# Second layer's routing in a fused two-layer kernel: first choice from the logits, weights computed last, half of an addition and of a norm on GpSimd, one dispatch split in two

## What is computed

```python
xn = _layernorm(x)
s  = attention(xn)                 # layer 0: 16 heads, causal
g  = silu(experts_top2(xn))        # layer 0: 8 experts
x  = x + s * g
xn = _layernorm(x)
s  = recurrent_attention(xn)       # layer 1: phases, cumulative sums, MLP
g  = silu(_L1_ffn_ref(xn))         # layer 1: 8 experts, capacity 64 per group of 256 tokens
x  = x + s * g
```

```python
raw = softmax(logits); idx1 = argmax(raw); gate1 = raw[idx1]
rest = raw * (1 - onehot(idx1)); idx2 = argmax(rest); gate2 = rest[idx2]
p1 = cumsum(m1) - m1                    # place of a token in its expert's buffer
p2 = cumsum(m2) - m2 + count(m1)
expert_inputs = einsum('GSEC,GSM->EGCM', dispatch, x)   # one-hot matmul, 8 groups of 256 tokens
```

## Time and profile before

| | us |
|---|---|
| three timed runs | 617.03, 617.17, 614.8; median 617.03 |
| the profiled run, device time | 616.33 |
| its span | 614.5 |
| busy in the span | TensorE 573.1, VectorE 476.7, ScalarE 330.9, GpSimd 190.4 |
| mean granted TensorE clock | 0.981 of full |

### The profile page before, as it was taken

The page is one execution under the profiler, slowest core; times in us unless marked ns, Lnnn a source line. Parts: engine busy times, 40 slices in busy tenths (PEclk is TensorE's granted clock), DMA queues, the critical chain, the costliest instruction groups (busy, mean ns, idle before and its releaser), DMA issues.

```text
span 614.5 us, 11961 instructions
## 1 busy us (share of the span) xinstructions
PE 573.1 (93%) x3901; PEld 352.2 (57%) x3902; DVE 476.7 (78%) x1307; ACT 330.9 (54%) x602; POOL 190.4 (31%) x221
## 2 busy tenths in 40 slices
PE   2878999999999999899999998989899999999996
PEld 1433544444444534899999963535446665656554
DVE  6799889999989898455555578666899899976465
ACT  2762567676777776555555558864223642362224
POOL 1451000000254452133333310000007685688300
PEclk9898899999999999999999999999999999999999
DMA  8955727070813171211111034215011322421412
GB/s 185 210 182 206 241 77 216 3 217 1 224 31 109 53 226 20 56 49 47 47 47 47 26 97 128 71 41 151 0 46 25 97 59 54 130 79 40 126 42 68
DMA packets 55612, 57.99 MB, mean 94 GB/s; under 512 B 8651, under 2 KB 39403, under 8 KB 55515
## 3 DMA queue, kind: packets, MB, share of 16 engines
q1 hardware_dynamic: 51242, 50.56, 29.9%
q0 software_dynamic: 4320, 6.81, 3.5%
HBM read 41.96 MB, written 18.85 MB: 99 GB/s over the span
## 4 chain that ended last, share of the span: by engine, by line
PE 76%; DVE 16%; ACT 4%; issue 2%; DMA 1%; SPq 1%; ACTq 0%; DVEq 0%
PE banks L1689 11%; PE banks L1831 10%; PE banks L1756 8%; PE banks L1778 7%; PE banks L1964 7%; PE banks L1701 6%; PE banks L1953 5%; PE banks L1950 5%; PE banks L2015 4%; DVE banks L1239 4%; DVE mpart L1242 3%; PE banks L1759 2%; ACT arena L809 1%; PE banks L1840 1%; PE banks L1598 1%
## 5 line engine op out<-in xcount | busy, mean ns | idle before, releaser
L809 ACT ACTIVATE arena<-banks 128x512 f32<-128x512 f32 (+1 forms) x304 | 154.3, 583 | 75.1 <-PE banks L1759 40.7
L1239 DVE CUSTOM_DVE_ANT_0 banks<-banks,arena 128x512 f32<-128x512 f32 (+3 forms) x256 | 119.7, 511 | 9.2 <-PE banks L1778 8.3
L1756 PE MATMUL banks<-arena 128*128 128x512 bf16 (+3 forms) x384 | 116.6, 331 | 4.0 <-ACT arena L809 2.8
L1778 PE MATMUL banks<-arena 96*128 96x512 bf16 (+3 forms) x384 | 113.5, 336 | 4.8 <-DVE mpart L1239 2.7
L1242 DVE TENSOR_REDUCE mpart<-banks 128x1 f32<-128x512 f32 x128 | 85.8, 683 | 9.1 <-PE banks L1778 8.1
L1689 PE MATMUL banks<-arena 128*128 128x128 f32 x624 | 76.3, 275 | 1.0 <-ACT arena L743 1.0
L1689 PEld LDWEIGHTS banks<-arena 128*128 128x128 f32 x624 | 72.8, 192 | 1.5 <-ACT arena L743 1.5
L1831 PE MATMUL banks<-arena 128*9 128x512 f32 (+3 forms) x768 | 70.7, 487 | 0.0
L851 ACT ACTIVATE arena<-banks 125x512 f32<-125x512 f32 (+2 forms) x48 | 28.4, 595 | 71.2 <-PE banks L1950 46.2
L1756 PEld LDWEIGHTS banks<-arena 128*128 128x128 bf16 x384 | 37.8, 99 | 49.6 <-issue 23.8
L620 POOL DMA_INDIRECT results<-arena x39 | 37.7, 967 | 77.4 <-DVE arena L1133 77.4
(11 more groups left out here) (295 smaller groups left out, 858.0 us busy)
## 6 DMA issues: line engine op xcount, KB each, us to landing
k_parts<-arena SPq DMA_DIRECT2D x6, 768.0 KB, 8.1
arena<-in_L_ffn_experts_w_dram SPq DMA_DIRECT2D x2, 2048.0 KB, 11.1
arena<-results SPq DMA_DIRECT2D x8, 512.0 KB, 6.6
arena<-k_parts SPq DMA_DIRECT2D x7, 576.0 KB
arena<-q_parts SPq DMA_DIRECT2D x28, 144.0 KB
arena<-in_L_ffn_w_kernel_dram SPq DMA_DIRECT2D x8, 344.0 KB, 3.8
slots<-in_pad_rows_dram SPq DMA_DIRECT2D x1, 2535.0 KB, 12.3
arena<-slots SPq DMA_DIRECT2D x39, 65.0 KB, 1.8
```

Source lines behind the costliest of these rows:

```text
L809: act.activation(Pr[:, r % 4, heads[0]:heads[-1] + 1, 0:n], ring_e[e % 3][:, 0:len(heads) * n].rearrange("p (j c) -> p j c", j=len(heads)) ...
L1239: ins = dve.tensor_tensor_reduce(unmasked, unmasked, tail_mask[:, 512 - n:512], 1.0, -BIG, ALU.add, ALU.max, part[:, at:at + 1])
L1756: ins = pe.matmul(ring_e[e % 3][:, at * n:at * n + n], QK[:, slot, j, 1, P * kt:P * kt + P], QK[:, slot, j, 0, q:q + n], start=True, stop= ...
L1778: ins = pe.matmul(ps[:, at * n:at * n + n], QK[0:TALL, slot, j, 0, P * i:P * i + P], QK[0:TALL, slot, j, 1, 512 * half:512 * half + n], st ...
```

## The change

Six edits are made.

1. `route_max` now also finds the one-hot of the first choice, from the logits and their maximum (the new function `first_equal`, which is `first_max` without its first step).
2. `route_choice` no longer divides the exponentials by their sum. It clears the first choice out of the raw exponentials and takes the second choice from what is left.
3. The weights of the two choices are computed by the new function `route_weights`, behind the four one-hot comparisons of each sequence.
4. The addition into `x1` for chunk 2 of the second sequence goes to GpSimd, which waits for VectorE's product (`ya_half`); VectorE waits for that addition (`x1_half`) before `norm_moments(1)`.
5. The last four of the eight rows of the norm (tiles 12 to 15) go to GpSimd, after `refine`; TensorE's transposes of chunk 3 wait for them (`xn1_last`).
6. On TensorE `dispatch(0)` is split: its first tile goes ahead of the last transposes of the attention, its second between them and the products with the output weights. `places1(1)` goes ahead of the eight one-column products.

```diff
@@ GpSimd
+            pool.wait_ge(Z["ya_half"], 1)
+            half = slice(QT, QT + QT // 2)
+            pool.tensor_tensor(x1[:, half, :], x1[:, half, :], ya[:, half, :], ALU.add).then_inc(Z["x1_half"], 1)
+            pool.wait_ge(Z["refined"], 2)
+            for n in range(QT + QT // 2, NT):
+                ins = pool.tensor_scalar(xn[:, n, :], x1[:, n, :], mv[:, n, 0:1], rstd[:, 2, n:n + 1], ALU.subtract, ALU.mult)
+            ins.then_inc(Z["xn1_last"], 1)
@@ VectorE, norm_rows
                     refine(slice(QT, NT))
+                    dve.sem_inc(Z["refined"], 1)
-                for n in range(QT * b, QT * b + QT):
+                for n in range(QT * b, QT * b + (QT // 2 if b else QT)):
@@ VectorE, routing
             def route_max(b):
-                R, r_, _ = halves(b)
+                R, r_, chosen = halves(b)
                 link(dve.tensor_reduce(r_[0], R[0], AX_X, ALU.max))
                 dve.tensor_tensor(R[1], R[0], over_experts(r_[0]), ALU.subtract).then_inc(Z["gates_d"], 1)
+                first_equal(R[0], r_[0], chosen[0], R[4], r_[4])
             def route_choice(b):
                 R, r_, chosen = halves(b)
                 dve.wait_ge(Z["gates_exp"], 2 + b)
-                link(dve.tensor_reduce(r_[0], R[1], AX_X, ALU.add))
-                link(dve.reciprocal(r_[1], r_[0]))
-                link(dve.tensor_tensor(R[0], R[1], over_experts(r_[1]), ALU.mult))
-                first_max(R[0], r_[0], chosen[0], R[4], r_[4])
-                link(dve.scalar_tensor_tensor(R[1], chosen[0], 0.0, R[0], ALU.is_equal, ALU.mult))
-                first_max(R[1], r_[1], chosen[1], R[4], r_[4])
+                link(dve.scalar_tensor_tensor(R[0], chosen[0], 0.0, R[1], ALU.is_equal, ALU.mult))
+                first_max(R[0], r_[1], chosen[1], R[4], r_[4])
                 dve.sem_inc(Z["selb_ready"], 1)
                 link(dve.scalar_tensor_tensor(R[3], chosen[0], 0.0, chosen[1], ALU.is_equal, ALU.mult))
+            def route_weights(b):
+                R, r_, _ = halves(b)
+                link(dve.tensor_reduce(r_[0], R[1], AX_X, ALU.max))
+                link(dve.tensor_reduce(r_[4], R[1], AX_X, ALU.add))
+                link(dve.reciprocal(r_[5], r_[4]))
+                link(dve.tensor_tensor(r_[0], r_[0], r_[5], ALU.mult))
+                link(dve.tensor_tensor(r_[1], r_[1], r_[5], ALU.mult))
@@ VectorE, the second sequence (route_weights(0) and (1) stand behind the one_hot loops)
-                link(dve.tensor_tensor(ya[:, tiles, :], ya[:, tiles, :], psM[...], ALU.mult))
-                link(dve.tensor_tensor(x1[:, tiles, :], x1[:, tiles, :], ya[:, tiles, :], ALU.add))
+                weighted = dve.tensor_tensor(ya[:, tiles, :], ya[:, tiles, :], psM[...], ALU.mult)
+                if c == 2:
+                    weighted.then_inc(Z["ya_half"], 1)
+                else:
+                    link(weighted)
+                    link(dve.tensor_tensor(x1[:, tiles, :], x1[:, tiles, :], ya[:, tiles, :], ALU.add))
+            dve.wait_ge(Z["x1_half"], 1)
             norm_moments(1)
@@ TensorE
+            dispatch(0, (0,))
             pe.wait_ge(Z["m_free"], READS)
...
+            dispatch(0, (1,))
...
-            for g in range(G1 // 2):
+            for g in range(1, G1 // 2):
                 dispatch(g)
             for c in range(2, 4):
-                pe.wait_ge(Z["xn1_ready"], c + 1)
+                pe.wait_ge(Z["xn1_ready"], 3)
+                if c == 3:
+                    pe.wait_ge(Z["xn1_last"], 1)
...
             phases(2)
+            places1(1, psM[:, 1, :])
             for o in range(2):
...
-            places1(1, psM[:, 1, :])
```

More of the change, by code:

```diff
@@ L373, in build @@
             r_done p2_done mem_set zero_o x2_done wg_ps wg_done el_done sqrt_in sqrt_out
-            y1_done disp_ps disp_sb oh_ready dest_in sin_done u1_ps g1_ps hid1_done act1_done gate_zero tail_zero xn1_ready refined full_sb r1_done rem1_done sum_in aT0_sb xT0_sb ld_vecs ld_iota"""
+            y1_done disp_ps disp_sb oh_ready dest_in sin_done u1_ps g1_ps hid1_done act1_done gate_zero tail_zero xn1_ready refined full_sb r1_done rem1_done sum_in ya_half x1_half xn1_last aT0_sb xT0_sb ld_vecs ld_iota"""
         Z = {n: sem(n) for n in names.split()}
@@ L950, in first_max, with first_equal @@
                 link(dve.tensor_reduce(best, values, AX_X, ALU.max))
+                first_equal(values, best, onehot, t1, t2)
+            def first_equal(values, best, onehot, t1, t2):
                 link(dve.tensor_tensor(t1, values, over_experts(best), ALU.is_equal))
@@ L1338, in _ @@
                             one_hot(g, oh0[:, 2 * g:2 * g + 2, :])
+                        route_weights(0)
             assert next(choice, None) is None and next(positions, None) is None
@@ L1345, in _ @@
                 dve.wait_ge(Z["s_ps"], c - 1)
-                link(dve.tensor_tensor(ya[:, tiles, :], ya[:, tiles, :], psM[:, c % 2, :].rearrange("p (n d) -> p n d", d=D), ALU.mult))
-                link(dve.tensor_tensor(x1[:, tiles, :], x1[:, tiles, :], ya[:, tiles, :], ALU.add))
+                weighted = dve.tensor_tensor(ya[:, tiles, :], ya[:, tiles, :], psM[:, c % 2, :].rearrange("p (n d) -> p n d", d=D), ALU.mult)
+                if c == 2:
[4 more added lines that the diff above has]
+            dve.wait_ge(Z["x1_half"], 1)
             norm_moments(1)
@@ L1358, in _ @@
                 one_hot(g, oh[:, 2 * g - 8:2 * g - 6, :])
+            route_weights(1)
             dve.wait_ge(Z["ld_L1"], 16 * 6)
@@ L1644, in places1, with dispatch @@
                 ins.then_inc(Z["pre_ps"], 1)
-            def dispatch(g):
+            def dispatch(g, tiles=(0, 1)):
                 pe.wait_ge(Z["oh_ready"], g + 1)
                 ps, source = (banks[:, g, :], oh0) if g < G1 // 2 else (psM[:, g % 2, :], oh)
-                for i in range(2):
+                for i in tiles:
                     ins = pe.matmul(ps, xn[:, 2 * g + i, :], source[:, (2 * g + i) % 8, :], start=(i == 0), stop=(i == 1))
-                ins.then_inc(Z["disp_ps"], 1)
+                if tiles[-1] == 1:
+                    ins.then_inc(Z["disp_ps"], 1)
             pe.wait_ge(Z["ld_spread"], 16)
```

## The result

The changed kernel takes 619.41 us (median of 20 runs, 616.85 to 623.51), the kernel before 616.44 (median of 20, 614.61 to 619.24). The ratio is 1.005, with a 95% interval of 1.0035 to 1.0064: 3.0 us slower, at the edge of what the prediction called no change. The forecast was 617.3, with a range of 614.9 to 619.9. The profiled run took 620.83 us (span 619.0), 4.50 more than the profiled run of before; 13 of the 20 runs were faster than it, so it shows more than the typical loss.

What follows compares the result with a forecast made beforehand. TensorE holds 76% of the chain that ended last, nearly without pause from dispatch 4 on. The six edits sum to -0.2 us and the clock adds 1.2: +1.0 on the profiled 616.33, so 617.3, range 614.9 to 619.9.

Steps and rivals of the forecast that it cites:

- likeliest case: All edits plus a fall to half clock partly on phases and dispatches: 617.3 us, range 616.3 to 618.2, chance 0.40.
- First sequence's routing: One-hot steps of the first choice fit into VectorE's wait for the exponential; gain 0.2 us, bounds 0 and 0.33.
- Dispatch 0 in two gaps: Its two tiles just fit TensorE's waits before the last transposes and output products; cost 0.1 us, bounds 0 and 0.4.
- Half of the addition: VectorE loses one 128x512 addition to GpSimd, but the two overlapping additions disturb each other; gain 0.35 us, bounds 0 and 0.7.
- Half of the rows on GpSimd: GpSimd's four norm rows end late and hold up chunk 3's transposes and logits; cost 1.3 us, bounds 1.0 and 1.9.
- Rival (c): VectorE's and GpSimd's norm rows exclude each other, chunk 3 0.9 us later; 617.0 at full clock, 618.2 with fall; chance 0.13.
- Second sequence's routing: On VectorE, ten steps instead of 14 and no 0.32 us wait before the second choice; gain 1.35 us.
- TensorE's order: `places1`, one-column products and two phases take 3.6 us before dispatch 4, so TensorE bounds its start, at 435.6.
- Weights at the end: `route_weights(1)` puts five short VectorE steps, some 1.15 us, ahead of the phases' reading; costs nothing, 0.4 us cover left.
- The clock: Longer light stretch on TensorE makes a 3.4 us fall on phases 0 and 3 and dispatches likely; cost 1.2 us.
- rival (b): The fall lasts twice as long, 6.5 us from about 432 on phases and dispatches, costing 3.2; 619.4 us, chance 0.12.
- the signs that the prediction named: Profile: no TensorE idle ahead of dispatch 4, logits copy 0.8 us later, choices 3.25 behind, half clock within 432 to 440.

Runs made afterwards that it cites:

- a4: Kernel before with only the routing edits, plus the semaphore increment ahead of the norm's rows; 0.9999 of the kernel before, 616.31 us.
- c2: Changed kernel with all eight norm rows back on VectorE, measured a second time; 0.9959 of the kernel before, 614.94 us.
- c4: Changed kernel with the counts (`places1`) behind the one-column products again; 1.0048 of the kernel before, 620.47 us.
- b4: Changed kernel with all norm rows on VectorE and three extra unread 512-column products on TensorE; 0.9992 of the kernel before, 618.66 us.
- a2: Changed kernel with dispatch 0 whole again, behind the output products; 1.0051 of the kernel before, 620.9 us.
- b2: Changed kernel with all norm rows on VectorE and dispatch 0 whole; 0.9975 of the kernel before, 617.67 us.
- a3: Changed kernel with three extra unread 512-column products in TensorE's waits for the norm's rows; 1.0000 of the kernel before, 617.5 us.
- a1: Changed kernel with all eight norm rows back on VectorE, first measurement; 0.9966 of the kernel before, 614.93 us.
- b3: Changed kernel with all norm rows on VectorE and the counts behind the one-column products; 0.9997 of the kernel before, 618.75 us.
- b1: Changed kernel with all norm rows and the whole addition on VectorE, first measurement; 1.0052 of the kernel before, 622.51 us.
- c1: Kernel before with one edit alone, the last four norm rows on GpSimd; 1.0032 of the kernel before, 619.25 us.
- c3: Changed kernel with all norm rows and the whole addition on VectorE, second measurement; 1.0003 of the kernel before, 618.28 us.

## Why the prediction came out as it did

The forecast was +1.0 us, in a range that reached to 619.9, and the measured median is +3.0. The time lies inside the range, but outside the 616.3 to 618.2 of the likeliest case. The parts, in the prediction's order:

- **First sequence's routing**, forecast -0.2. The last transposes of the lists start at 411.67 instead of 411.90: -0.23. This pair agrees, but it is not shown by more than the pair: a4, c2, c4 and b4, which have the edit too, have them at 411.55 to 412.16, and the kernel before stands in the middle of that.
- **Dispatch 0 in two gaps**, forecast 0.1. The last transposes of the attention start at 413.05 and the output products at 414.87, 0.05 later than a shift of 0.23 gives. Right, and a2 and b2 show that the split is worth nothing else.
- **Half of the addition**, forecast -0.35. GpSimd's step took 1.27 us (1.155 in rows 6) and VectorE's own 0.97 (0.69 before): the two did disturb each other. The moments begin 2.62 us behind VectorE's first product, 0.27 sooner than before (2.89). The Trainium skill's rule of a full block (SBUF — State Buffer, "Who interferes with whom") would have made VectorE's step end at GpSimd's end plus its own 0.69, 418.18 + 0.69 = 418.87; it ended at 418.72, so this trace comes near the rule without meeting it, and GpSimd, which had begun first, was slowed too.
- **A wait that the prediction left out.** `dve.sem_inc(refined)` stands ahead of VectorE's rows, which now start 0.23 us after the last short step, where they started 0.04 after it: 0.2 us. a4, which has this wait and both additions on VectorE, shows it alone (its row at 422.96 above has the same 0.23): 8.20 us from the first output product to T instead of 8.01. It eats most of the addition's gain, which is 0.27 by itself (8.20 to 7.93); T came out 0.08 earlier, not 0.35.
- **Half of the rows on GpSimd**, forecast T + 3.6 for their end and T + 6.0 for the logits. They ended at T + 3.1 (422.73 + 3.17), four steps of 0.79 and a start of 0.16 behind `refine`, with no disturbance beyond VectorE's four rows taking 1.28 us in place of 1.07. Rival (c), rows that exclude each other, did not happen. The transposes started at T + 3.25, and the logits nevertheless came at T + 6.5, since the 8-column products ran at half clock. With the clock full, in a3, they came at T + 5.6, which is the delay's own price: 0.9 us more than before, where the forecast was 1.3.
- **Second sequence's routing**, forecast -1.35. From the copy of the logits to the end of the second one-hot it is 3.18 us in place of 4.59: -1.4. Right; but TensorE's order let none of it through until the counts were moved (a4).
- **TensorE's order**, forecast 3.6 us from the counts to dispatch 4 at full clock. It was 3.8 to 3.9 in a1, b2 and c2. TensorE is the bound there, as forecast, and VectorE's one-hot no longer waited for.
- **Weights at the end**, forecast nothing: the experts waited for the copy of the last dispatch. Right; in a4 and b3, where dispatch 4 is not behind, they waited 0.85 us instead of 0.77, for VectorE.
- **The clock**, forecast a half clock of 3.4 us of which 1.2 are lost. This is the term that was mis-sized. It lasted 13.7 us in the changed kernel's profile, and it took 3.4 us between the counts and dispatch 4 (7.28 in place of 3.87), 0.4 behind it and 0.9 in the logits. A fall of the forecast's length and place, in a3, cost 1.6. The mechanism was named, in the forecast and more so in rival (b), where it was given 6.5 us, 3.2 us of loss and a chance of 0.12. The median came out at rival (b)'s 619.4 (its own terms give 616.33 - 0.2 + 3.2 = 619.3), and that is in part luck: (b) has the clock fall at about 432 for 6.5 us, where it fell at 427.24 for 13.7, and the profiled run lost 4.5 us, not 3. The stretch at 45 us that (b) was taken from lasts 6.8 us by the reckoning used here (45.12 to 51.94), not 6.5.

Of the signs that the prediction named, GpSimd's steps, the choices and the missing idle time ahead of dispatch 4 came out. The copy of the logits came 1.53 us later than 427.78, not 0.8, and the half clock began at 427, not at 432.

Where that step failed: it asked where the next fall would come and, in its forecast, took for granted that it lasts 3.4 us, because phases 1 and 2 had ended the one of before. In the table of the profiles they end it only where they begin with it. Where the phases start up to 0.6 us after the fall (before, a1, a4, b2, b3, b4, c2) the half clock lasted 3.4 us in all seven. Where they start 0.8 us after it or later (the changed kernel, a2, b1, c1, c3, c4) it lasted 6.8 us in one and 13.7 in five. As the profiles read, the rows on GpSimd do most of their harm by moving the phases 1.9 us later (they start at T + 4.4 in a1, at T + 6.3 in the changed kernel), out of the place in which they ended the fall; 1.1 of it is the late transposes, the rest 8-column products already at half clock. That a cause so small has such an effect is shown by a1 and c2 on one side and a3 on the other; the exact point, between 0.6 and 0.8 us, rests on one profile each side. The length does not grow with the distance either: c1, with 2.6 us the farthest, has the 6.8. Why the half clock then lasts so long is not shown, nor what sets the moment at which a fall begins.

The best kernel found is a1: the change without its GpSimd rows, 0.9966 and 0.9959 of the kernel before in two measurements on two chips. Both intervals lie below 1, and it beats both kernels.

## What to carry to other kernels

Moving work to an idle engine must be priced at that engine's rate and at the place where its last piece is awaited: four rows that VectorE does in 1.07 us took GpSimd 3.17, and TensorE stood idle for 1.26 us for the last of them. On TensorE the cost of a wait is not its length: when light pieces and gaps stand in a row, look at the granted clock, and ask which heavy work will end the fall, not only where the fall begins. A fall on work beside a longer chain of another engine cost nothing here, the same fall on the critical work 1.6 us. A shortened chain pays only up to the next engine in order behind it: the routing's 1.4 us were worth nothing until the counts were moved ahead of the one-column products.

## What the runs showed of the hardware

- TensorE stayed at half clock for 13.7 us while its rows say busy 1.00 in every microsecond of it. Half-clocked phases, one-column products, phases and dispatches did not lift it at once; before, 3.4 us of the same phases did.
- Three unread products of 512 columns, put into waits, took the changed kernel from 1.005 to 1.0000 of the kernel before.
- The runs of one kernel stand on levels 1.4 to 1.9 us apart (the kernel before on the chip of a1: 614.5 to 615.1, 616.3 to 617.1, 617.7 to 618.3, 619.8 to 619.9, one run between at 618.9, with mean granted clocks of mostly 0.984, 0.981, 0.975 and 0.972). One such step lies far ahead of the change: every profile has three or more half-clock stretches in its first 65 us, and the six profiles in which the first and the last of them took 3.4 us each reach the last transposes of the lists at 409.7 to 410.8, the eight in which one of the two took 6.8 us at 411.5 to 412.6. So a single profile shows one of several courses, and a median moves when the share of the levels does.
- VectorE's addition with both inputs in SBUF took 0.97 us beside GpSimd's of the same form, and GpSimd's took 1.27 in place of 1.155.
